# Three PSUM bank pairs in turn for the first 28 units, a reordered SyncE program and a later last addition, in a fused attention and feed-forward kernel

## What is computed

```python
def ada(x, g, b):   return (t @ g.T)[:, None, :] * rmsnorm(x) + (t @ b.T)[:, None, :]
def attention(x):   # 16 heads, softmax(scale * q k^T) v, then W_o
def swiglu(x):      return silu(x @ gate_w.T) * (x @ hidden_w.T) @ out_w.T + out_b
x = x + (t @ attn_alpha_w.T)[:, None, :] * attention(ada(x, attn_gamma_w, attn_beta_w))
x = x + (t @ ffn_alpha_w.T)[:, None, :]  * swiglu(ada(x, ffn_gamma_w, ffn_beta_w))
x = layernorm(x) * weight + bias + tanh(t @ lin_w.T + lin_b)[:, None, :]
return x * weight + bias
```

## Time and profile before

| | |
|---|---|
| median of 3 runs | 765.31 us (764.29 to 766.41) |
| the profiled execution | 765.27 us, of which span 763.5 us |
| mean granted TensorE clock over the span | 0.988 of 2.4 GHz |
| TensorE busy | 715.5 us, 94% |
| VectorE busy | 536.7 us, 70% |
| ScalarE busy | 471.2 us, 62% |
| GpSimd busy | 392.2 us, 51% |
| units 0 to 27 | 37.58 to 146.57 us |

### The profile page before, as it was taken

One profiled execution on the slowest core, in us unless ns is written; L12 is line 12 of the kernel. 1 busy time (PEld: TensorE's weight loads), 2 busy tenths in 40 slices (PEclk: granted clock), 3 DMA queues, 4 the chain that ended last, 5 costly groups with the idle time before them and its releaser, 6 DMA issues.

```text
span 763.5 us, 17526 instructions
## 1 busy us (share of the span) xinstructions
PE 715.5 (94%) x6660; PEld 489.1 (64%) x6660; DVE 536.7 (70%) x797; ACT 471.2 (62%) x860; POOL 392.2 (51%) x493
## 2 busy tenths in 40 slices
PE   6698889899999999999999999999999999999995
PEld 5433334467676667676767677766676667678894
DVE  4777777777677866777686767767777776436765
ACT  4357677786666766675667756666665665743431
POOL 4354142543376634855367543856267454872533
PEclk9879999999999999999999999999999999999998
DMA  7577566365434644265444554255343640232210
GB/s 225 167 209 241 174 217 215 104 213 169 148 102 140 188 134 167 65 211 147 137 157 138 176 149 153 60 196 153 126 148 120 187 108 5 79 103 60 56 43 29
DMA packets 63132, 107.18 MB, mean 140 GB/s; under 512 B 10464, under 2 KB 18072, under 8 KB 63048
## 3 DMA queue, kind: packets, MB, share of 16 engines
q1 hardware_dynamic: 61892, 104.79, 43.6%
q10 hardware_dynamic: 1028, 1.07, 0.5%
q0 software_dynamic: 128, 0.20, 0.1%
HBM read 57.50 MB, written 37.52 MB: 124 GB/s over the span
## 4 chain that ended last, share of the span: by engine, by line
PE 73%; DVE 10%; issue 7%; ACT 6%; DMA 3%; POOL 1%; ACTq 0%; POOLq 0%; DVEq 0%
PE ps_x L1391 17%; PE ps_j L1278 12%; PE ps_o L1364 12%; PE ps_s L1351 10%; PE ps_j L1404 10%; PE ps_m L1336 7%; DVE mx L1096 3%; ACT prob L892 3%; PE ps_o L1404 2%; DVE fx L1062 2%; DVE gate_t L1136 2%; DMA prob<-in_wk 1%; PE ps_m L1391 1%; PE ps_s L1391 1%; DVE act_y L1143 1%
## 5 line engine op out<-in xcount | busy, mean ns | idle before, releaser
L1096 DVE TENSOR_REDUCE mx<-ps_m 128x2 f32<-128x1024 f32 x222 | 271.7, 1224 | 118.5 <-PE ps_m L1336 118.0
L892 ACT ACTIVATE prob<-ps_s 128x1024 f32<-128x1024 f32 x256 | 262.0, 1024 | 75.4 <-PE ps_s L1351 72.8
L1364 PE MATMUL ps_o<-prob,v 128*32 128x512 f32 x1024 | 137.2, 608 | 0.2 <-ACT o_raw L900 0.2
L1351 PE MATMUL ps_s<-qs,ks 64*128 64x512 f32 x512 | 119.8, 464 | 18.1 <-ACT prob L892 14.1
L1351 PEld LDWEIGHTS ps_s<-qs,ks 64*128 64x128 f32 x512 | 48.4, 185 | 135.7 <-issue 76.8
L1391 PE MATMUL ps_x<-n,gh_hi 64*128 64x256 f32 x872 | 97.7, 284 | 1.7 <-DVE act_y L1143 1.6
L607 POOL TENSOR_TENSOR a_lo<-act_y,a_hi 128x256 fp32r<-128x256 f32 x100 | 73.6, 737 | 46.6 <-ACT a_hi L923 46.4
L1336 PE MATMUL ps_m<-ks,qs 64*128 64x512 f32 x444 | 91.7, 409 | 6.1 <-DVE mx L1096 4.2
L1391 PE MATMUL ps_x<-n_x,gh_hi 64*128 64x256 f32 x872 | 94.3, 276 | 0.0
L632 POOL TENSOR_TENSOR xr<-xr,sc 128x512 f32<-128x512 f32 x41 | 53.2, 1298 | 59.5 <-DVE sc L1108 40.5
L1391 PEld LDWEIGHTS ps_x<-n,gh_hi 64*128 64x128 f32 x872 | 74.2, 184 | 13.7 <-DVE act_y L1143 10.2
(11 more groups left out here) (182 smaller groups left out, 1441.1 us busy)
## 6 DMA issues: line engine op xcount, KB each, us to landing
qs<-stack_scratch SPq DMA_DIRECT2D x30, 512.0 KB, 4.6
ks<-stack_scratch SPq DMA_DIRECT2D x30, 512.0 KB, 6.8
stack_scratch<-qk_hi SPq DMA_DIRECT2D x56, 256.0 KB, 3.1
out_scratch<-o_raw SPq DMA_DIRECT2D x32, 256.0 KB, 3.5
n_x<-n SPq DMA_DIRECT2D x32, 256.0 KB, 3.7
stack_scratch<-qk_lo SPq DMA_DIRECT2D x28, 256.0 KB, 3.4
on_lo<-out_scratch SPq DMA_DIRECT2D x16, 256.0 KB
d_c<-reciprocal_scratch SPq DMA_DIRECT2D x16, 256.0 KB
```

The lines of the kernel that those rows point to most:

```text
L892: act.activation(prob[:, n % 2, 2 * h:2 * h + 2, :], ps_s[:], ACT.Exp, scale=SCALE).then_inc(p_r, 1)
L1096: dve.tensor_reduce(mx[:, group % 2, :, h, qt], max_pair(mp)[:], AX.X, ALU.max).then_inc(mx_red, 1)
L1351: mm = pe.matmul(ps_s[:, s, :], ks[r:r + 64, g, j, kb * P:(kb + 1) * P], qs[r:r + 64, g, j, :], start=True, stop=True)
L1364: mm = pe.matmul(ps_o[32 * i:32 * i + 32, :], v[:, g, kb, i, :], prob[:, n % 2, i, :], start=(kb == 0), stop=(kb == TT - 1), skip_group_ch ...
```

## The change

Four edits.

1. In units 0 to 27 every pair of matmuls, S or M, takes the next of three bank pairs: `turn` lists them in TensorE's order (S0, M0, S1, M1, and one M more in units 0 and 1) and number k goes to `(ps_s, ps_m, ps_x)[k % 3]`. A pair waits for whoever read the pair three turns earlier: an S usually for a reduction on VectorE, an M usually for an exponential on ScalarE.
2. SyncE, units 16 to 19: `stack_read(1, 3)` goes from the start of unit 16 to behind `o_read(0, 1)` in unit 18; `rec_write(0, 1)` goes ahead of `stack_write(2, 0)` and `rec_read(0, 1)` stays behind it; the load of x for the second half of batch 0 goes behind `rec_read(0, 1)`.
3. GpSimd's last addition of `weigh(7, 0)` also waits for the last `a_lo` on VectorE.
4. The last store is two DMAs of one token tile each, on SyncE and on ScalarE's queue, each behind its own step of `last_norm`.

```diff
+        turn = []
+        for n in range(GH_AT):
+            maxima = list(early_maxima(n))
+            turn += [("S", 2 * n), ("M", maxima[0]), ("S", 2 * n + 1)] + [("M", mp) for mp in maxima[1:]]
+        turn_no = {what: no for no, what in enumerate(turn)}
...
+            return (ps_s, ps_m, ps_x)[no % 3]
...
+        def store_last(queue, t):
+
+            queue.wait_ge(z_last_r, 3 + t)
+            queue.dma_start(dram["out"][B - 1][:, 2 + t, :], xr[:, (B - 1) % 2, 2 + t]).then_inc(out_w[1][(B - 1) % 2], 16)
...
-                if at(0, 0) and b > 0:
+                if at(0, 0) and b > 1:
                     stack_read(b, 3)
...
                 if n == UNITS + 2:
                     o_read(0, 1)
+                    stack_read(1, 3)
...
-                if at(3, -1):
+                if at(3, -1) and b > 1:
                     load_xr(b - 1, 1)
+                if n == UNITS + 3:
+                    rec_write(0, 1)
                 if at(3, 1):
                     stack_write(b + 1, 0)
-                if n == UNITS + 4:
-                    rec_write(0, 1)
+                if n == UNITS + 3:
                     rec_read(0, 1)
+                    load_xr(0, 1)
...
+                if hf == 2 * B - 2:
+                    pool.wait_ge(a_tail_r, NE - TAIL)
                 pool.tensor_tensor(xs, xs, tab_b[:].unsqueeze(1).broadcast_to([P, 2, D]), ALU.add).then_inc(z_r, 1)
...
+            def wait_turn(kind, i):
+
+                no = turn_no[kind, i] - 3
+                if no >= 0 and turn[no][0] == "S":
+                    pe.wait_ge(p_r, turn[no][1] + 1)
+                elif no >= 0:
+                    pe.wait_ge(mx_red, turn[no][1] + 1)
+                else:
+                    pe.wait_ge(mx_red, LEAD_IN + no + 1)
```

More of the change, by code:

```diff
@@ L231, in early_maxima, with in_turn, score_pair, last_in @@
             return range(2 * (n + LEAD), 2 * (n + LEAD) + 2)
-        def max_pair(mp):
-            return (ps_m, ps_x)[mp % 2] if mp < 2 * (GH_AT + LEAD) else ps_m
+        turn = []
[3 more added lines that the diff above has]
+        turn_no = {what: no for no, what in enumerate(turn)}
+        def in_turn(no):
+            return (ps_s, ps_m, ps_x)[no % 3]
+        def score_pair(n, j):
+            return in_turn(turn_no["S", 2 * n + j]) if n < GH_AT else ps_s
+        def max_pair(mp):
+            if mp < LEAD_IN:
+                return (ps_m, ps_x)[mp % 2]
+            return in_turn(turn_no["M", mp]) if mp < 2 * (GH_AT + LEAD) else ps_m
+        def last_in(kind, bank):
+            return max(i for no, (k, i) in enumerate(turn) if k == kind and in_turn(no) is bank)
         def gh_banks(e):
@@ L430, in store @@
             def store(b, h):
[L431 to L434, removed]
+                if 2 * b + h == 2 * B - 1:
+                    store_last(sp, 0)
+                    return
+                sp.wait_ge(z_r, 4 * (2 * b + h + 1))
                 sp.dma_start(dram["out"][b][:, 2 * h:2 * h + 2, :], xr[:, b % 2, 2 * h:2 * h + 2]).then_inc(out_w[h][b % 2], 16)
@@ L541, in _ @@
                 for u in range(2):
-                    sp.wait_ge(out_w[h][u], 16 * (B // 2))
+                    sp.wait_ge(out_w[h][u], 16 * (B // 2 + (h == 1 and u == (B - 1) % 2)))
         @block.gpsimd
@@ L891, in exps @@
                     act.wait_ge(av_done, n - 1)
-                act.activation(prob[:, n % 2, 2 * h:2 * h + 2, :], ps_s[:], ACT.Exp, scale=SCALE).then_inc(p_r, 1)
+                act.activation(prob[:, n % 2, 2 * h:2 * h + 2, :], score_pair(n, h)[:], ACT.Exp, scale=SCALE).then_inc(p_r, 1)
             def o_evac(b, g):
@@ L1035, in _ @@
                 unit(n)
+            store_last(act, 1)
         @block.vector
@@ L1329, in max_scores @@
                     pe.wait_ge(stack_in[g], 32 * reads(b + 1, g))
-                if 2 <= mp < 2 * (GH_AT + LEAD):
+                if 2 <= mp < LEAD_IN:
                     pe.wait_ge(mx_red, mp - 1)
+                elif LEAD_IN <= mp < 2 * (GH_AT + LEAD):
+                    wait_turn("M", mp)
                 elif mp >= 2 * (GH_AT + LEAD):
@@ L1344, in scores @@
                     pe.wait_ge(m_in, 32 * (NG * b + g + 1))
-                if n + j > 0:
+                if n + j == 0:
+                    pe.wait_ge(v_st_r, 2)
+                elif n < GH_AT:
+                    wait_turn("S", 2 * n + j)
+                elif n >= GH_AT:
                     pe.wait_ge(p_r, 2 * n + j)
-                else:
-                    pe.wait_ge(v_st_r, 2)
+                if n == GH_AT and j == 0:
+                    pe.wait_ge(mx_red, last_in("M", ps_s) + 1)
                 for s in range(2):
                     r = 64 * s
-                    mm = pe.matmul(ps_s[:, s, :], ks[r:r + 64, g, j, kb * P:(kb + 1) * P], qs[r:r + 64, g, j, :],
+                    mm = pe.matmul(score_pair(n, j)[:, s, :], ks[r:r + 64, g, j, kb * P:(kb + 1) * P], qs[r:r + 64, g, j, :],
                                    start=True, stop=True)
```

## The result

The changed kernel takes 759.07 us (median of 4 runs, 758.29 to 759.93) against 765.86 for the kernel before beside it (4 runs): ratio 0.9912, 95% interval 0.9887 to 0.9937. 759.9 (757.0 to 762.6) was predicted. The profiled execution took 758.38 us, its span 756.5 (before 765.27 and 763.5), at a mean granted clock of 0.988 in both.

What follows compares the result with a forecast made beforehand. A loop of waits sets the pace in units 0 to 27, TensorE bounds the stretch from unit 28. Edits 1 to 4 give 4.1 + 0 + 1.06 + 0.2 = 5.4 us off 765.27: 759.9 us, range 757.0 to 762.6.

Steps and rivals of the forecast that it cites:

- the twelve units without a large job: Units 2, 6 to 10, 14, 15, 17, 18, 22, 26: each gains 0.33 us from edit 1, 4.0 in all.
- The loop of 2.94 us: Job-free units: exponential of S1, next M0, attend, next S1, exponential again; 2.94 us per unit, where a unit took 3.27.
- more gain behind large jobs: Units 6, 14, 22, 26, following a large job: 0.35 us more each, 1.4 us, from partly overlapping a copy out of `ps_j`.
- The twelve large-job units: Units 3 to 5, 11 to 13, 19 to 21, 23, 24, 27: about 0.12 us for four of them, 0.5 us.
- The three places it runs into: Unshrinking paths take back edit 1's gain: maxima's DMAs before S0(8) 0.8 and S0(28) 0.4, W_o to FT 0.6 us.
- It keeps the reciprocals ahead of W_o: Edit 2, SyncE's order: no gain of its own in the old pace; taken as 0, bounds 0 and 1 us lost.
- The landing: Reciprocals' write on SyncE: between 1.4 and 4.3 us in the trace, taken as 2.7; ring order would put it near 4.3.
- the limit: Sign of being wrong: scores in the changed profile wait for reductions for more than some 3 us.
- That rival: Scores get hung on VectorE's reductions in 27 units, costing 8 us: 2.7 us slower overall, 768.0 us; chance 0.04.
- Transfers hold more: DMA waits at units 4, 8, 16, 28 and the reciprocals eat 2 us more: edit 1 gives 2.1, 761.9 us; chance 0.20.

Runs made afterwards that it cites:

- e3: The changed kernel with SyncE's old order (edits 1, 3 and 4 without edit 2): ratio 0.9946, giving up 1.9 of the 6.0 us gain.
- e1: Edit 1 alone (the bank pairs) against the kernel before: 1.7 us gained by the ratio, 2.5 by the medians.
- e10: The changed kernel with the stacked read of group 3 back at the start of unit 16, the rest of edit 2 kept: ratio 0.9916.
- e4: The changed kernel without the wait of GpSimd's last addition (edit 3 undone): 4.4 of the 6.0 us won, by the ratios.
- e8: The changed kernel with the last store one again, on SyncE (edit 4 undone): time not distinguishable from the changed kernel's; last normalization to end 3.40 us.
- e6: The changed kernel with attend whole between S1 and M1 in TensorE's order: 3.5 us longer than the changed kernel, 2.7 by the ratios.
- e9: The changed kernel with one weight piece issued behind the maxima's rows of group 2 instead of right ahead of them: ratio 0.9934.
- e5: The changed kernel with attend split into two halves around M1 in units 1 to 27: each half holds TensorE 0.98 us; total time not given.
- e7: The changed kernel with the three pairs fixed, S0 on ps_s, S1 on ps_m, every M on ps_x: 22 us slower than changed, 15 than before.

## Why the prediction was right, point by point

**Edit 1** was forecast at 4.1 us and the early units gave 4.23, but the runs say that this is edits 1 and 2 together: with the old order of SyncE only part of it arrives (e3, e1). By kinds of unit, from M0 to M0: the twelve units without a large job went from 42.04 to 37.64 us, 4.4 against 4.6 forecast (5.4 less 0.8 for S0(8)). (From S0 to S0 it is 42.26 to 36.36, and the large-job units pay the difference.) The loop of 2.94 us is there to the hundredth in units 6, 8, 14 and 22 (2.93 or 2.94). In units 2, 10, 15 and 18 it is 3.02 to 3.05: there M0 itself started after a wait or held up, and needs 0.41 to 0.43 to the next instruction (75.19 to 75.62), for which I had put 0.33. Unit 9, which I had named at 2.9, takes 3.29, and 3.19 from S0 to S0: there attend starts 0.58 behind M0 and not 0.43, as ScalarE copies `ps_o` until 72.34, and M0(10) comes 0.1 later than the exponential lets it. Against that stood more gain behind large jobs (unit 6 3.68 to 2.94; unit 26, which I had counted with them, follows none and still went from 4.11 to 3.42). The twelve large-job units lost 0.4 (49.12 to 49.49); forecast was -0.5 (0.5 less 0.4 less 0.6). Unit 13 takes 4.09; I had said about 4.2.

**The three places it runs into** came out nearly to the number. MT(6) to S0(8) takes 4.43 us (forecast 4.29), MT(26) to S0(28) 4.97 (4.87), W_o to FT 132.80 - 123.74 = 9.06 (9.1), each ended by what was named. Unit 28 starts at 141.25; I had said near 142.4, and 1.1 of that is the earlier start, which no edit made.

**Edit 2** is the step that failed. "It keeps the reciprocals ahead of W_o" at 0, bounded by 0 and 1 lost, left out a gain; e3 shows 1.9 us in the times and 2.6 in the profiles. I had seen that they were just in time and that units 17 to 22 would get shorter, and did not put the two together. The path has little to give: in the kernel before, `o_norm` ended at 125.53 and `on_hi` started at 126.28 without a wait, 0.75 us to spare, and in the new pace with the old order `on_hi` waits 1.32 us (e3). I also looked at W_o as the first to wait, where it is `on_hi` in ScalarE's queue, ahead of two exponentials. The forecast of the total held because it silently counted edit 1 with this path intact; in that it was lucky, since a change with edit 1 and without edit 2 would have been forecast at the same 4.1 us and gave 1.7 to 2.5 (e1).

The landing, which I took as 2.7, was 4.14 us (3.82 in the second profile), and M1 of unit 23 waits 0.4 us there, which it does not in e10. The Trainium skill, DMA: Bandwidth & Descriptors, section Queues, rings and completion order, says that on each DMA engine descriptors are consumed in ring order. The trace agrees where the megabyte is: 4.14 with it, 2.39 without it (e10). It does not account for 2.78 before and 4.31 in e3 with the same order ahead.

**Edit 3**: 1.06 forecast, 1.07 on `a_lo` and 1.15 to the end measured. The Trainium skill, SBUF — State Buffer, section SBUF: two separate sides, says that a VectorE instruction with two SBUF inputs and a GpSimd instruction that reads SBUF exclude each other for the whole instruction; the trace agrees, 1.50 beside it in e4 and 0.43 without, and the scaling with an input in PSUM stayed at 0.69.

**Edit 4**: 0.2 forecast, 0.27 between the two profiles (3.44 to 3.17), 0.15 to 0.23 against e8; visible in e8's profile, not in its time.

**Not forecast**: 1.09 us at the start, which both kernels show by themselves, and 0.34 in the middle, which is within what it varies by. Without the start the profiles differ by 5.9; 5.4 was forecast.

**The rivals.** Scores waited 0.78 us for reductions where I had set 3 as the limit. That rival is real, as e6 shows, and lies one attend away. "Transfers hold more" did not decide, but transfers took what e9 had won.

## What to carry to other kernels

Buffers in turn over two kinds of users gain only if the order of the instructions gives each buffer's slowest reader its time; of three pairs fixed to their users, one plan was 6 us and another 22 us slower than the same three in turn. When a change makes a stretch shorter, go through every path that was just in time there and ask whether it gets shorter too, and look for the first instruction queued behind its arrival, not for the one that uses it. Where the DMA engines are full behind a wait that a transfer ends, expect a new order of transfers to move it on.

## What the runs showed that was not expected

- Half of attend, two of four products that write 32 columns each, held TensorE for 0.98 us, the whole for 0.99 (e5).
- After 3.12 us in which TensorE idled, the granted clock fell to 1.2 GHz for 6.8 us (e1); in e3 it fell, for 3.4 us, after an idle 1.47 us and 1.5 us of matmuls. Behind the 1.50 us ahead of S0(8) in the changed kernel it stayed at 2.4 GHz. So a wait in this kernel can cost more than its length.
- The same 16 KB write landed in 2.39 to 5.24 us: 3.8 to 4.1 with a megabyte of reads right ahead of it, 2.39 without (e10), but also 2.8, 4.3 and 5.2 behind the same row of DMAs (before, e3, e1).
- The start of the early stretch differs by some 2 us between profiles of kernels with the same start (S0(0) at 36.0 to 38.1), and unit 1 takes 3.4 to 4.9 us (5.7 in e7), according to when the clock rises to 2.4 GHz.
